# A cross-attention encoder layer on one core: z and q through DRAM, the last group's z on TensorE, weights and rows by GpSimd's queue

## What is computed

```python
q = (query @ Wq + bq).reshape(b, s, N_HEADS, D_K).transpose(0, 2, 1, 3)
k = (key @ Wk + bk).reshape(b, s, N_HEADS, D_K).transpose(0, 2, 1, 3)
v = (values @ Wv + bv).reshape(b, s, N_HEADS, D_K).transpose(0, 2, 1, 3)
scores = jnp.einsum('bhqd,bhkd->bhqk', q, k) / jnp.sqrt(jnp.float32(D_K))
scores = jnp.where(j < i + mask, scores, NEG_INF)      # mask == 0
attn = jax.nn.softmax(scores, axis=-1)
attn = attn.at[:, :, 0, :].set(0.0)
ctx = jnp.einsum('bhqk,bhkd->bhqd', attn, v)
attn_out = ctx.transpose(0, 2, 1, 3).reshape(b, s, d) @ Wo + bo
x = layer_norm(query + attn_out, ln1_g, ln1_b)
ffn = jax.nn.relu(x @ W1 + b1) @ W2 + b2
out = layer_norm(x + ffn, ln2_g, ln2_b)
```

## Time and profile before

| | us |
|---|---|
| median of 3 runs | 1664.28 (1663.89 to 1666.03) |
| the profiled execution, its own time | 1661.53 |
| its span, first to last instruction | 1659.6 |
| TensorE busy in the span | 1616.8 |
| ScalarE busy | 1547.8 |
| VectorE busy | 1436.3 |
| GpSimd busy | 1381.1 |

### The profile page before, as it was taken

The page is one execution under the profiler, slowest core; times in us unless marked ns, Lnnn a source line. Parts: engine busy times, 40 slices in busy tenths (PEclk is TensorE's granted clock), DMA queues, the critical chain, the costliest instruction groups (busy, mean ns, idle before and its releaser), DMA issues.

```text
span 1659.6 us, 54093 instructions
## 1 busy us (share of the span) xinstructions
PE 1616.8 (97%) x16700; PEld 1590.2 (96%) x16700; DVE 1436.3 (87%) x6746; ACT 1547.8 (93%) x5905; POOL 1381.1 (83%) x1352
## 2 busy tenths in 40 slices
PE   4799999999999999999999999999999999999998
PEld 3699999999999999999999999999999999999997
DVE  3788898898898898898898898898898898898885
ACT  3899999999999999999999999999999999999993
POOL 2378888888888888888888888888888888888896
PEclk7799999999999999999999999999999999999999
DMA  8856665656656656656665666755666656665630
GB/s 153 173 121 119 133 136 117 134 131 120 134 135 117 135 132 119 135 132 119 134 136 116 135 132 118 136 133 116 135 134 117 136 133 118 136 135 117 122 76 27
DMA packets 307087, 208.99 MB, mean 126 GB/s; under 512 B 164336, under 2 KB 281968, under 8 KB 306800
## 3 DMA queue, kind: packets, MB, share of 16 engines
q1 hardware_dynamic: 304960, 204.47, 60.5%
q10 hardware_dynamic: 1840, 1.05, 0.3%
HBM read 104.73 MB, written 50.33 MB: 93 GB/s over the span
## 4 chain that ended last, share of the span: by engine, by line
PE 95%; DVE 2%; ACT 1%; SPq 1%; DMA 1%; issue 0%; POOL 0%; DVEq 0%; ACTq 0%; POOLq 0%
PE ps_dense L393 32%; PE ps_dense L404 32%; PE ps_probsT L500 14%; PE ps_scores L490 7%; PE ps_att L518 7%; PE ps_dense L375 2%; ACT probs L595 0%; DVE ps_scores L804 0%; DMA q_stack<-qT 0%; DMA probs<-in_L_xattn_Wk_dram 0%; SPq L253 0%; PE ps_att L417 0%; SPq L247 0%; SPq L269 0%; SPq L290 0%
## 5 line engine op out<-in xcount | busy, mean ns | idle before, releaser
L595 ACT ACTIVATE probs<-ps_scores,negmax 128x128 f32<-128x128 f32 x2048 | 744.1, 413 | 8.5 <-DVE negmax L804 5.2
L1059 POOL TENSOR_TENSOR probs<-probs,recip 128x512 f32<-128x512 f32 x512 | 533.1, 1042 | 134.7 <-DVE recip L787 134.5
L804 DVE CUSTOM_DVE_ANT_0 ps_scores<-ps_scores,mask 128x128 f32<-128x128 f32 x2048 | 527.0, 318 | 69.9 <-PE ps_scores L490 67.7
L595 ACT ACTIVATION_READ_ACCUMULATOR probs<-ps_scores,negmax 128x1 f32 x2048 | 517.3, 253 | 0.0
L404 PE MATMUL ps_dense<-w,hT 128*128 128x256 f32 x3048 | 417.9, 286 | 0.9 <-DVE u L929 0.9
L393 PE MATMUL ps_dense<-zT,w 128*128 128x256 f32 x3072 | 416.9, 285 | 0.9 <-DVE h_f L888 0.5
L1067 POOL TENSOR_TENSOR hT<-h_f,hT 128x512 fp32r<-128x512 f32 x252 | 322.8, 1294 | 90.4 <-DVE h_f L888 90.4
L393 PEld LDWEIGHTS ps_dense<-zT,w 128*128 128x128 f32 x3072 | 381.8, 189 | 1.5 <-issue 0.9
L404 PEld LDWEIGHTS ps_dense<-w,hT 128*128 128x128 f32 x3048 | 377.5, 188 | 1.2 <-DVE u L929 1.1
L612 ACT ACTIVATE probsT<-ps_probsT 128x508 f32<-128x508 f32 x512 | 319.4, 624 | 37.4 <-PE ps_probsT L500 37.4
L500 PE MATMUL ps_probsT<-ident,probs 128*128 128x128 f32 x2048 | 313.1, 275 | 0.0
...
## 6 DMA issues: line engine op xcount, KB each, us to landing
...
q_stack<-qT SPq DMA_DIRECT2D x762, 64.0 KB, 2.0
k_spill<-kT SPq DMA_DIRECT2D x128, 256.0 KB, 2.2
c_tok<-in_ctx_dram SPq DMA_DIRECT2D x256, 64.0 KB, 5.0
x_res<-in_x_dram SPq DMA_DIRECT2D x64, 256.0 KB, 3.0
x_tok<-in_x_dram SPq DMA_DIRECT2D x252, 64.0 KB, 2.4
out_dram<-o_tok SPq DMA_DIRECT2D x63, 256.0 KB, 2.7
...
```

Of the source, the lines that this page charges most:

```text
L595: last = nc.scalar.activation(probs[:, m % 4, i, :], ps_scores[m % 2][:, i, :], ACT.Exp, bias=negmax[:, m % 4, i:i + 1], scale=-1.0, accum ...
L804: last = nc.vector.tensor_tensor_reduce(ps_scores[m % 2][:, i, :], ps_scores[m % 2][:, i, :], mask[:], -1.0, -MASKED, ALU.add, ALU.min, ac ...
L1059: nc.gpsimd.tensor_tensor(probs[:, m % 4], probs[:, m % 4], recip[:, m % 4, :].unsqueeze(2).broadcast_to([P, 4, S]), ALU.mult)\
```

## The change

1. q: instead of twelve copies from SBUF to SBUF, `spill_q` writes its two halves to DRAM (2 DMAs of 256 KB) and `stack_q` reads them back with 3 DMAs of 256 KB per group. Group 0 keeps its direct copies.
2. z: for all groups but the last, `spill_z` writes `u1` to DRAM, `load_z` reads it in 32-row blocks (4 DMAs) into the tile of `x_res`, `z_flips` transposes it there in 32x32 blocks on DVE, and `z_hi` and `z_lo` split it from SBUF. The four PE transposes go. The next residual may be loaded only after `z_lo`. The last group's z is still transposed on PE, by 16 narrow products (`last_z`) into a scores bank.
3. Because of the block order, rows of W1 and the columns g1 and be1 are loaded by block: eight small DMAs, issued by SP ahead of the second x.
4. W1, six of the seven rows and W2 are issued by POOL's queue after its memsets. Wv, Wo and the row bv are issued by SP at the start; their splits come before the first group.
5. v of group 0 is projected before the first iteration, q of a group one iteration earlier than before (`q_project(it + 3)`).
6. All five orders, `BANK` and `HELD_BY` are written anew.
7. The last norm works in `y_b2` with the statistics of norm 1.

```diff
-BANK = {"zT": 2, "v": 0, "q": 2, "f1_0": 2, "k": 0, "f1_1": 1, "f1_2": 2, "f1_3": 0, "wo": 1, "f2": 1}
+BANK = {"v": 2, "q": 1, "f1_0": 2, "k": 2, "f1_1": 1, "f1_2": 0, "f1_3": 2, "wo": 2, "f2": 0}
...
+            def spill_q(g, part):
+                if exists(g) and g > 0:
+                    if part == 0:
+                        sp.wait_ge(s_hi["q"], KC * (g + 1))
+                    else:
+                        sp.wait_ge(taken["q"], KC * (g + 1))
+                    need(sp, s_qstack, 16 * PARTS * (g - 2))
+                    sp.dma_start(q_dram[g % 2, part].rearrange("c p t -> p c t"), f32(qT[:, part])).then_inc(s_qspill[part], 16)
+
+            def stack_q(g, part):
+                if exists(g) and g > 0:
+                    sp.wait_ge(s_qspill[part], 16 * g)
                     need(sp, s_scores, (g - 1) * UNITS)
                     for s, half in enumerate(QPART):
...
+                        if half == part:
+                            sp.dma_start(f32(q_stack[g % 2][32 * s:32 * s + 32]), q_rows[g % 2, part]).then_inc(s_qstack, 16)
...
             def load_residual(g):
                 if exists(g):
-                    if g == 0:
-                        load_weight(5)
-                    need(sp, taken["wo"], g)
+                    need(sp, s_zlo, g)
                     sp.dma_start(x_res[:], x_v[g]).then_inc(s_xres, 16)
+
+            def spill_z(g):
+                if exists(g) and g < NG - 1:
+                    sp.wait_ge(s_z1, GB * (g + 1))
+                    need(sp, s_zrow, 16 * 4 * (g - 1))
+                    sp.dma_start(z_dram[g % 2].rearrange("b s d -> s b d"), u1[:]).then_inc(s_zspill, 16)
+
+            def load_z(g):
+                if exists(g) and g < NG - 1:
+                    sp.wait_ge(s_zspill, 16 * (g + 1))
+                    sp.wait_ge(taken["wo"], g + 1)
+                    for j in range(4):
+                        sp.dma_start(z_tile[32 * j:32 * j + 32], z_blocks[g % 2, j]).then_inc(s_zrow, 16)
...
             def iteration(it):
-                stack_k(it + 2, 0)
-                next_c(it + 4)
-                stack_q(it + 3, 0)
+                spill_k(it + 3, 0)
+                stack_q(it + 3, 1)
                 load_residual(it + 1)
-                stack_q(it + 3, 1)
-                spill_k(it + 3, 0)
                 spill_k(it + 3, 1)
+                stack_k(it + 3, 0)
+                stack_k(it + 3, 1)
                 store(it - 2)
-                next_x(it + 5)
-                stack_k(it + 3, 1)
+                spill_q(it + 4, 0)
+                next_c(it + 5)
+                spill_z(it + 1)
+                spill_q(it + 4, 1)
+                stack_q(it + 4, 0)
+                load_z(it + 1)
+                next_x(it + 7)
...
             def z_hi(g):
-                if exists(g):
-                    take_hi("zT", zT, g, full["f1_3"], g)
+                if g == NG - 1:
+                    act.wait_ge(s_zlast, 1)
+                    act.wait_ge(full["f1_3"], g)
+                    nc.scalar.activation(zT[:, 0].rearrange("p c t -> p (c t)"), z_last, ACT.Copy).then_inc(s_hi["zT"], 1)
+                elif exists(g):
+                    act.wait_ge(s_zflip, g + 1)
+                    need(act, full["f1_3"], g)
+                    nc.scalar.activation(zT[:, 0].rearrange("p c (o t) -> p c o t", t=32), z_by_chunk(), ACT.Copy)\
+                      .then_inc(s_hi["zT"], 1)
...
+            def z_flips(g):
+                if exists(g) and g < NG - 1:
+                    dve.wait_ge(s_zrow, 16 * 4 * (g + 1))
+                    nc.vector.transpose(z_tile, z_tile).then_inc(s_zflip, 1)
...
+            by_block = WEIGHTS[4][0].rearrange("(j c d) n -> j d c n", j=4, c=KC)
+            for j in range(4):
+                nc.gpsimd.dma_start(RAW[4][0][0][32 * j:32 * j + 32], by_block[j]).then_inc(s_w[4], 16)
+            for dram, tile in ROWS[1:]:
+                nc.gpsimd.dma_start(tile, dram.rearrange("(a n) -> a n", a=1).broadcast_to([P, D])).then_inc(s_wr, 16)
+            by_chunk = WEIGHTS[5][0].rearrange("(c p) n -> p c n", p=P)
+            for raw, c, n in RAW[5]:
+                nc.gpsimd.dma_start(raw, by_chunk[:, c:c + n, :]).then_inc(s_w[5], 16)
```

361 lines of the change are left out of this document (195 added, 166 removed).

## The result

The changed kernel takes **1672.04 us** (median of 5 runs, 1671.55 to 1674.13) against 1664.28 us (1663.27 to 1666.03) for the kernel before on the same chip: ratio 1.0053, 95% interval 1.0043 to 1.0064. It is 0.5% slower, where 1640 us was forecast. The profiled execution took 1672.82 us, of which the span is 1671.0.

A forecast was written before the change was run, and what follows sets the result against it. TensorE's instruction stream was taken as the bound. Against the profiled 1661.53 us, -27.7 (transposes), +2 (stalls) and +1.3 (start) gave 1637.1; the runs' median lies 2.75 higher, so 1640 us, range 1631 to 1658.

The forecast's parts named there:

- -27.7 us for the transposes: Middle: 63 of 64 groups lose four z transposes from TensorE, 0.44 us per group, so the period falls to 24.42 us.
- the 0.03 us for new stalls: Middle: new TensorE waits per period, put near none because banks are taken over a block or more later; +2 us.
- the block price of 1.42 us: Middle: each TensorE block of twelve products was priced at 1.42 us.
- VectorE 23.05 us: Middle: VectorE's work per period, 22.21 plus 0.70 for z's transpose and 0.14 for z's low part, under 24.42.
- The form of rival 1 on VectorE: Middle: z's low part, 0.90 us longer, delays maxima and exponentials; passing on 0.2 us gives 1653; whole rival 0.18 plus 0.06.
- ScalarE's form: Middle: ScalarE, at 24.03 to 24.17 us, sets the pace, 1651 or 1664; chance with VectorE's case 0.18 plus 0.06.
- The start, +1.3 us with +8 as the worst: Start: later first maxima +3.3, removed splits and waits -4.4, less TensorE work in the third group +2.4; sum +1.3 us.
- taken as hidden: Start: GpSimd's 14 load issues cost nothing, since GpSimd idles 14.95 us before the first normalisation.
- The bounds of -6 and +8: Start: -6 us with gains and no delay, +8 us with no gains, the delay and SP's extra issues.
- the lighter fill: Start: the third group has three up products and no down product instead of four and two; +2.4 us.
- The end, neutral within 1.3 us: End: more products cover the last normalisation, nothing covers z's two last copies; no net change, bound 1.3 us either way.
- Rival 2, the z loop: Middle: z's trip through DRAM into the residual's tile, 23.1 us, may reach 25.7 and set the period; 1718 us, chance 0.14.

The follow-up runs named there:

- e18: Changed kernel with bulk loads in SP's queue behind the small transfers, moments ahead of the reciprocals, and 64 unused bytes in front of aT: 1647.04 us.
- e9: Changed kernel with each norm's moments issued ahead of the reciprocals on VectorE, nothing moved between engines: 1669.43 us.
- e1: Changed kernel with GpSimd waiting until group 0's q stacks have landed before it issues W1, six rows and W2: 1667.71 us.
- e5: Changed kernel with W1, W2 and six rows in SP's queue, each behind the small transfers that something waits for: 1661.58 us.
- e6: Changed kernel with the low parts of h of group 62 on VectorE, as those of group 63: 1671.87 us.
- e2: Changed kernel with W1, W2 and six rows back in SP's queue, where the kernel before had them: 1675.12 us.

## Why the prediction was wrong, point by point

- **What bounds the kernel** was right: TensorE's stream. "TensorE busy throughout" was seen too, and it misled: a pause of 0.07 us and blocks of up to 1.46 us instead of 1.42 don't show in that column.
- **-27.7 us for the transposes** was right as a price and wrong as a sum. Per period 0.437 us left. The twelve product blocks grew by 17.14 - 16.93 = 0.21, the slot by 0.08, the scores shrank by 0.08 (2.207 to 2.124, means of the same view): 0.23 us remained, and **the steps that failed are the 0.03 us for new stalls, of which the slot alone took 0.07, and the block price of 1.42 us taken as constant**. The stall was put near none because a bank is taken over only after another block or more; k's bank waits for VectorE all the same, because VectorE comes to `h_full` late. With 64 bytes of shift in both kernels and VectorE relieved in both, the change gives 24.767 - 24.353 = 0.41 us: the mechanism holds, near its size. That tile addresses set block times is shown. Why the changed order's blocks are longer at the same addresses is not. Two things fit and weren't isolated: v's block stood behind q's before (1.363 us) and stands behind an up block now (1.430), and e18 shows that a neighbour's tile can move it; and blocks right ahead of transposes take 1.437 us before and 1.430 to 1.462 after, of which there is one before and five after. Start-to-start distances can also pass time from a block to the scores next to it, so blocks and scores together, +0.13, are the firmer number.
- **VectorE 23.05 us** was the size missed: 24.08 (391.14 of 400 us, x 24.63). z's low part +0.59 instead of +0.14, xT's +0.24, and the two eps operations 0.6 longer each, which no term held (operations overlap on the engine, so that these sum to more than the difference). The form of rival 1 on VectorE had the right route, a VectorE operation held by a GpSimd pass that makes TensorE late, at 0.06 to 0.08 us per period instead of 0.2, but named the wrong operation: in e9 z's low part is as long as before and the wait is gone with that of eps. ScalarE's form did not come, its load is 23.88 us.
- **The start, +1.3 us with +8 as the worst,** was +13.9. The failed step is "taken as hidden" for W1, W2 and the rows: it priced 14 issues (0.55 to 0.73 us each, done at 30.04 us, so that part was right) and not the 2.88 MB behind them, which held up group 0's q stacks, x of group 2 and, by e1, the spill of q. In my own rows the first 85 us had a DMA share of 0.84. The half of the Trainium skill's rule that I left out, that the transfers interleave, was the one that decided. Without the collision (e5) A1 is 2.2 us later than before, so the rest of the sum is right as a total; its terms weren't told apart, except the first maxima, 2.9 us later in e5 against 3.3. The bounds of -6 and +8 don't come out of their own terms: no gains, delay, SP's 4 us and the lighter fill are +9.7.
- **The end, neutral within 1.3 us,** was +10.3. The deeper pipeline leaves four more blocks behind the last attention product (4 x 1.42 = 5.7 us of work that periods and start no longer hold), waits of 4.95 us instead of 1.81, and the last z's narrow transposes in 1.08 us instead of 0.66. That is 9.3 of the 10.3 us. I counted the lighter fill as +2.4 us of wait, and not its price at the end. The failed step is the one that took the end as neutral. e6 shows that one wait taken away is replaced by the next, and the stretch is 40.9 to 41.7 us in every form of the changed kernel; what the depth costs as such wasn't tried.
- **Rival 2, the z loop,** did not bind in the changed kernel: one wait of 0.7 us for z's blocks in 1300 us. Its sum of landings was too careful or the slack enough; the run doesn't tell which. In e18 it binds in single periods.
- **DMA share** 0.78 to 0.84 in the middle, as forecast (0.73 to 0.91). First maxima 46.62 us against 36; at 36 in e1, e2 and e5.

Predicted 1637.1 for the profiled execution, 1672.8 came. By span the three misses are 12.6 (start), 12.9 (middle, -12.8 for -25.7) and 10.3 us (end).
